# The transpose of an attention's negated maxima, moved one step further behind the chain that splits them

## The reference, cut to what matters

```python
scores = jnp.einsum('bqhd,bkhd->bhqk', q, k) / jnp.sqrt(jnp.float32(dh))
attn = jax.nn.softmax(scores, axis=-1)
out = jnp.einsum('bhqk,bkhd->bqhd', attn, v).reshape(B, Lq, H)
return x_q + (out @ Wp + bp)          # layer 0: attention over the context
...
h = mha(q, k, v) @ self_o_w + self_o_b      # layer 1: over the 112 tokens themselves
x = x + h * gate_msa
h = layer_norm(x, norm2_g, norm2_b)
h = mha(h @ q_w + q_b, k_ctx, v_ctx) @ cross_o_w + cross_o_b   # then over the context
x = x + h
...                                          # then an MLP of width 1024
```

## Time and profile before

| | |
|---|---|
| time, median of 3 runs | 572.43 us (568.38 to 573.84) |
| profiled execution | 572.44 us, of which the span of its instructions 570.6 us |
| PE busy | 459.4 us, 81% of the span |
| PEld busy | 335.9 us, 59% |
| DVE, ACT, POOL busy | 255.7 us (45%), 245.1 us (43%), 261.2 us (46%) |
| granted PE clock, mean | 0.93 of full speed |

### The profile page before, as it was taken

The page is one execution under the profiler, slowest core; times in us unless marked ns, Lnnn a source line. Parts: engine busy times, 40 slices in busy tenths (PEclk is TensorE's granted clock), DMA queues, the critical chain, the costliest instruction groups (busy, mean ns, idle before and its releaser), DMA issues.

```text
span 570.6 us, 11962 instructions
## 1 busy us (share of the span) xinstructions
PE 459.4 (81%) x4446; PEld 335.9 (59%) x4446; DVE 255.7 (45%) x682; ACT 245.1 (43%) x537; POOL 261.2 (46%) x406
## 2 busy tenths in 40 slices
PE   0554768696989999997878877989789888989996
PEld 0532447464666576675756645666456655669885
DVE  0520724345456555554464464556346556611111
ACT  0121133343555655555443444555354554565220
POOL 5354643877596573544456337553223423153000
PEclk9995858788799999999897899999799999999999
DMA  8723521323244434346223413335422131100001
GB/s 207 160 74 110 133 78 38 102 63 84 75 129 103 122 95 109 81 133 184 66 64 81 105 38 91 97 98 133 126 75 77 43 83 48 37 3 0 17 17 34
DMA packets 74788, 48.71 MB, mean 85 GB/s; under 512 B 38969, under 2 KB 71697, under 8 KB 74729
## 3 DMA queue, kind: packets, MB, share of 16 engines
q1 hardware_dynamic: 64580, 37.82, 26.0%
q10 hardware_dynamic: 10148, 10.11, 6.1%
HBM read 17.27 MB, written 0.93 MB: 32 GB/s over the span
## 4 chain that ended last, share of the span: by engine, by line
PE 58%; DVE 11%; POOL 10%; DMA 8%; issue 5%; SPq 3%; ACT 3%; ACTq 0%; POOLq 0%; DVEq 0%
PE bank L573 9%; DVE nmax L941 8%; PE bank L579 7%; PE bank L524 7%; DMA q_stack<-nm_t 6%; PE bank L479 6%; PE bank L498 6%; PE bank L596 5%; PE bank L643 5%; PE bank L633 4%; PE bank L545 3%; POOL ctx_norm L1133 3%; PE bank L533 2%; POOL x_norm L1145 2%; SPq L881 1%
## 5 line engine op out<-in xcount | busy, mean ns | idle before, releaser
L941 DVE TENSOR_REDUCE nmax<-bank 112x1 f32<-112x375 f32 x256 | 127.7, 542 | 155.6 <-PE bank L498 155.5
L711 ACT ACTIVATE prob<-bank 125x448 f32<-125x448 f32 (+1 forms) x224 | 119.9, 543 | 127.5 <-PE bank L479 108.0
L479 PE MATMUL bank<-q_stack,k_stack 99*128 99x112 bf16 x768 | 71.4, 219 | 22.2 <-DMA q_stack<-nm_t 14.1
L498 PE MATMUL bank<-k_stack,q_stack 96*128 96x375 bf16 x256 | 73.7, 339 | 18.4 <-DVE nmax L941 8.6
L479 PEld LDWEIGHTS bank<-q_stack,k_stack 99*128 99x128 bf16 x768 | 50.6, 101 | 45.6 <-DMA q_stack<-nm_t 17.9
L573 PE MATMUL bank<-ctx_t,wkv 128*128 128x375 f32 x128 | 58.4, 588 | 2.8 <-ACT ctx_t L732 1.8
L498 PEld LDWEIGHTS bank<-k_stack,q_stack 96*128 96x128 bf16 x256 | 25.2, 100 | 56.0 <-DVE nmax L941 35.1
L1139 POOL TENSOR_SCALAR x_veps<-x_mv 112x1 f32<-112x1 f32 x32 | 7.4, 231 | 102.7 <-DVE x_mv L935 102.0
L1150 POOL CAST k_parts<-k_rest 128x375 bf16<-128x375 f32 x32 | 15.9, 497 | 78.3 <-DVE k_rest L991 78.3
L524 PE MATMUL bank<-prob,v_tokens 125*17 125x112 f32 x1536 | 51.1, 267 | 0.1
L579 PE MATMUL bank<-wkv,ctx_t 128*125 128x256 f32 x192 | 50.3, 399 | 0.2 <-DVE k_rest L991 0.2
(11 more groups left out here) (114 smaller groups left out, 744.6 us busy)
## 6 DMA issues: line engine op xcount, KB each, us to landing
k_stack<-k_parts SPq DMA_DIRECT2D x192, 93.8 KB, 2.2
q_stack<-job_part SPq DMA_DIRECT2D x144, 56.0 KB, 2.0
ctx_tokens<-in_ctx_dram ACTq DMA_DIRECT2D x14, 375.0 KB
k_self_stack<-job_part SPq DMA_DIRECT2D x48, 56.0 KB, 2.2
late_space<-in_L_xcond_mlp_w_dram ACTq DMA_DIRECT2D x2, 1024.0 KB, 5.5
late_space<-in_L_xcond_ada_w_dram SPq DMA_DIRECT2D x1, 1536.0 KB, 6.3
gate_self<-gate_rows SPq DMA_DIRECT2D x8, 112.0 KB, 3.1
k_self_stack<-gate_rows SPq DMA_DIRECT2D x1, 896.0 KB, 6.9
```

What stands on the lines that cost most here:

```text
L479: last = pe.matmul(sh.score_t[n % 2][:, j * T:(j + 1) * T], keys, sh.q_all[:, b, o:o + T], start=True, stop=True)
L498: last = pe.matmul(bank[:, 0:L], sh.q_all[0:DEEP, b, place(k) * T:place(k) * T + P], sh.k_st[i % 2][0:DEEP, k, 0:L], start=True, stop=True)
L711: act.activation(sh.prob[n % NPROB][0:rows, :], sh.score_t[n % 2][0:rows, 0:GH * T], ACT.Exp, scale=SCALE).then_inc(sg.exp_done, 1)
L941: dve.tensor_reduce(sh.nmax[i % 2][:, place(k):place(k) + 1], sh.score[n % 2][0:T, 0:L], AX_X, ALU.max, negate=True).then_inc(sg.max_done, 1)
```

## The change

The transpose of the negated maxima of an attention (fill N) moves one step back for 22 of the 24 attentions: from step 9 to step 10 of the stage before for attentions over the context, from step 1 to step 2 for attentions 10 to 16. The places of attentions 8 and 9 stay. The chain and the maxima stay where they are. `NM_AT`, and with it the issue of the transfer, is derived from `N_AT` and moves by one step too: to step 11 and to step 3, the last step of the stage. The order in which fills take the two banks follows the order of the fills, so it changes also.

```diff
     if i_ == 2 * B:
...
-        CHAIN_AT[i_], N_AT[i_] = (15, 0), (15, 1)
+        CHAIN_AT[i_], N_AT[i_] = (15, 0), (15, 2)
     elif cross(i_):
         MAX_AT[i_] = [(i_ - 1, k // 2) for k in range(H)]
-        CHAIN_AT[i_], N_AT[i_] = (i_ - 1, 8), (i_ - 1, 9)
+        CHAIN_AT[i_], N_AT[i_] = (i_ - 1, 8), (i_ - 1, 10)
...
     else:
-        MAX_AT[i_], CHAIN_AT[i_], N_AT[i_] = [(i_ - 2, k) for k in range(4)], (i_ - 1, 0), (i_ - 1, 1)
+        MAX_AT[i_], CHAIN_AT[i_], N_AT[i_] = [(i_ - 2, k) for k in range(4)], (i_ - 1, 0), (i_ - 1, 2)
```

## The result

The changed kernel takes 596.86 us (595.61 to 599.08, 4 runs), the kernel before 570.75 us over all runs so far (4): a ratio of 1.046, with a 95% interval of 1.039 to 1.053. It is slower, as forecast, but by 26 us and not by 13, and outside the range. The profiled execution has a span of 597.3 us against 570.6 us, 26.7 us more, and the granted clock is 0.897 in the mean, not 0.93.

The account below looks back on a forecast made before the run. The path through the maxima's transfer was taken as the bound: PE waits 14.1 us for its landing, 15.0 us for the transpose's chain. 10.8 + 4.0 + 2.8 + 0.3 − 8.0 + 3.1 = 13.0 us gave 585.4 us, range 577 to 594.

Parts of the forecast that it names:

- The issue hangs on the scores of step 11: Context stages: ACT's issue of the maxima's transfer follows step 11's scores, which begin 1.33 us behind step 10's.
- The second context transpose waits for ACT's read: Ahead of attentions 4, 5, 17, 19, 20, 21: changed bank order starts that transpose 0.5 us later.
- The gain in the stages of four steps: Attentions 10 to 16: 11.0 us of chain waits go, 3.0 us of landing waits appear, gain 8.0 us.
- Attention 3: Boundary ahead of attention 3: later issue and bank wait, but less slowing by other transfers, cost 1.3 us.
- costs of 4, 5 and 17: Stages with context transposes: later scores plus bank wait, 1.8 us each, six such attentions, 10.8 us in all.
- PE's clock. Net 3.1 us: Granted clock: four new falls of 1.76 us, 7 us, less three that go, 3.9 us.
- cost 2: Attentions 6, 7, 22, 23, without context transposes: issue 1.0 us later each, no bank wait, 4.0 us in all.
- 2.27 us, all of it transfer: Context boundaries: time from issue of the maxima's transfer to the next stage's scores, taken as 2.27 us of transfer.
- cost 4: Attention 18: the small transfer's end is tied to the 896 KB transfer's, so the later issue costs only 0.3 us.
- The early part: Attentions 0, 1 and 2: POOL's context norm partly hides the later starts, 0.5 us each, 1.5 us in all.
- C: Rival: PE's clock falls at nearly every boundary, seven times, without recovery in four-step stages, 594.3 us; chance 0.17.
- Rival B: ACT's issue isn't held by scores and goes once the copy is done: faster, 565.0 us; chance 0.06.

Follow-up runs that it names:

- e4: Kernel before the change, transposes unmoved, only the issue of the maxima's transfers one step later: 607.80 us, ratio 1.061.
- e5: Changed kernel with the transfers of the maxima issued in the step of their transpose, not one step later: 557.65 us, ratio 0.978.
- e8: Changed kernel with only the transposes of attentions 10 to 16 moved and every maxima transfer issued in its transpose's step: 554.82 us, ratio 0.969.
- k4: Changed kernel with two idle matmuls ahead of PE's wait for the maxima of attentions 18 to 23: 585.28 us, ratio 1.021.
- e1: Changed kernel with the 1 MB transfer of MLP weights issued in step 11 of stage 6, not step 10: 592.54 us, ratio 1.037.
- e3: Changed kernel with only the context attentions' transposes moved, those of attentions 10 to 16 back at step 1: 606.51 us, ratio 1.062.
- e6: Changed kernel with four idle matmuls ahead of PE's wait for the maxima of attentions 18 to 23: 590.67 us, ratio 1.034.
- e7: Changed kernel with SP's second six key transfers released by the next stage's first scores: 590.29 us, ratio 1.033.
- e10: The e8 kernel with SP's 896 KB gates transfer at step 5 of stage 18, not step 8 of stage 17: 550.53 us, ratio 0.959.
- e2: Changed kernel with only the transposes of attentions 10 to 16 moved, the context attentions' back at step 9: 564.16 us, ratio 0.987.

## Why the prediction was wrong, step by step

In the table, predicted terms are those of the prediction's sum; the measured ones are the differences between the profiled executions in the distances from one attention's start to the next.

| part | predicted | measured |
|---|---|---|
| up to attention 2 | +1.5 | +3.4 |
| attentions 3 to 6 | +1.3 +3.6 +1.0 | +6.4 |
| attention 7 | +1.0 | +6.5 |
| attentions 8 and 9 | 0 | +2.2 |
| attentions 10 to 16, with the low stretches that go | −8.0 −3.9 | −12.0 |
| attentions 17 and 18 | +1.8 +0.3 | +1.8 −1.0 |
| attention 19 to the end | +5.4 +2.0 +7.0 | +19.4 |
| sum | +13.0 | +26.7 |

**Right.** The issue hangs on the scores of step 11: it comes 0.40 to 0.42 us after their beginning at every context attention from 2 on, and e4 and e5 show that this is nearly the whole cost (e8 puts the transpose's own at 0.6 to 0.7 us a stage). The second context transpose waits for ACT's read (0.28 us late, 0.76 us early in the program, 5.2 us in all). The gain in the stages of four steps came as forecast, with landing waits of 0.78, 0.46, 0.62, 0.43 and 0.76 us in five of seven. That its sum fits to 0.1 us is in part luck: of the three falls of the clock counted as gone two went (299.5 and 316.6 us), and the third, at 354 us before, is at 355 us now. Attention 3 and the costs of 4, 5 and 17 were met within 0.35 us.

**Wrong, first: "PE's clock. Net 3.1 us".** This is the step that failed. It counted four new falls of 1.76 us, 7.0 us. From attention 19 on there are five new ones (all six boundaries from 18 to 23 have one, instead of one boundary), and each costs 2.08 us (k4): 10.4 us. Low stretches at 246, 270 and 287 us, where before there was one at 272 us, cost some 4.7 us more. So new falls cost about 15 us and not 7, and these 8 us are the largest part of the 13.7 us by which the forecast missed the profiled difference of 26.7 us. The 1.76 us were the difference of two stages of the kernel before that also differ in how much else PE waits, and weren't measured by themselves. Every boundary from 18 to 22 idled about 2.56 us, and the clock fell at each. With 0.5 to 0.9 us of idle time and two matmuls in it, it fell at none. What else decides it stays open: it didn't fall after 2.58 us in e4, and it did after 1.58 us ahead of attention 22 in e5.

**Wrong, second: cost 2 at attention 7.** I counted how far the issue moves, and not past what. The prediction looked at the context load that now stands right behind L821 on ACT; it missed the 1 MB of weights that now stands ahead of it (e1). The excess is 5.5 us there. The transfer is 2.9 us of it, the wait of 4.54 us against 1.65 in e1. About 2.5 us are the low stretch from 246 to 253 us, which comes before the 1 MB is issued and which e1, e3 and e6 don't have, though their order of work is the same up to there: bad luck, as far as is known. The low stretch at 270 us, right behind the long wait, and the longer one at 287 us make up the 2.2 us at attentions 8 and 9; in e1, without the long wait, these 2.2 us are gone.

**Wrong, third and smaller: "2.27 us, all of it transfer".** With SP's six transfers of keys released by the same scores it is 2.52 us, at ten boundaries (e7). The same event now starts both queues.

**Attention 18.** The prediction let the small transfer end with the 896 KB one, however late it is issued. In the changed kernel it took 2.52 us (the prediction expected 3.5), issued 4.4 us behind the large one, and the boundary came out 1.0 us better. e10 shows that the large one is what costs there: a latency of 6.07 us with it near and 2.26 without. But the end of the small one isn't tied to the landing of the large one, as cost 4 had it. In e5 the large one was issued at 381.61 and took 7.4 us, to 389.0, and PE had the maxima at 387.05:

```profile
381.61 0.59 SPq L1280 DMA_DIRECT2D k_self_stack<-gate_rows  x1
383.49 0.73 ACTq L821 DMA_DIRECT2D q_stack<-nm_t  x1
387.05 0.37 PE L479 MATMUL bank<-q_stack,k_stack 99*128 99x112 bf16 x4 [2.02 <-DMA q_stack<-nm_t]
```

```profile
k_self_stack<-gate_rows SPq DMA_DIRECT2D x1, 896.0 KB, 7.4
```

So the two landings of the kernel before, 0.3 us apart, were no proof. The rule that the prediction took from the Trainium skill (page "DMA: Bandwidth & Descriptors", section "Queues, rings and completion order") speaks of one DMA engine at a time, and no run here tells it from shared bandwidth; which of the two it is stays open.

**The early part** (+1.9 us over the forecast) isn't explained by the change alone: attention 1's start lies between 115.9 and 119.1 us in kernels that have the same order up to there (e3, e6), and e2, with nothing changed there, shows +2.7 us.

**The rivals.** C (the clock falls at nearly every boundary) is what happened from attention 18 on, but the stages of four steps recovered, as they did in the forecast; the time is above C's 594.3 us too. Rival B, that ACT's issue isn't held by scores, is false for the change, but made true in e5 it gives 557.7 us, against the 565 us that B gave.

## What to carry to other kernels

When an instruction is moved by a step, list what its followers are moved past on each queue. Here the transpose cost little where it was moved ahead of context attentions, and gained in the stages of four steps; its transfer, tied to it by a table, was moved behind the last scores of the stage, a 1 MB load and six transfers of another queue. A transfer wants to be issued when its data is ready, not behind work that has nothing to do with it. And a wait that grows from 1 to 2.5 us on PE costs more than 1.5 us: here the fall of the clock, which came at nearly every such wait, cost 2.08 us on top, more than the wait's own growth.

## What the runs showed of the hardware that I hadn't expected

- With a wait of 2.56 us ahead of each stage, the granted clock was at 1.2 GHz for 6.8 us, of which the first 0.4 to 1.2 us lay in the wait, and the stage took about 2 us more, five stages in a row. Two matmuls of 512 float32 columns (1.94 us at that place) in the wait kept 2.4 GHz. In e4 the clock stayed at 2.4 GHz after one such wait of 2.58 us.
- A transfer of 10.5 KB took 5.40 us, from its issue to PE's start, behind a 1 MB transfer issued 1.1 us ahead of it on the same queue, and 2.52 us when it was issued 1.0 us ahead of it.
- Six transfers of 94 KB on another queue, begun at the same moment, added 0.25 us. An 896 KB transfer on that queue, issued 1.2 to 1.9 us ahead of the small one, brought it to between 3.57 and 6.07 us (the kernel before, e2, e5, e7 and e8).
- ACT issues a transfer without waiting until the exponential ahead of it in the list has run, but only once the scores that this exponential waits for are done: 456.57, 0.04 us after their end at 456.53. The list is held by the waits in it, not by the work.
